# First expert layer of a vision tower: from every expert on every token to gathered tiles of 128 rows

## The chip, the cores and the metric

One core of a Trainium2 chip (trn2) runs the whole model in one launch. The metric is the device time of one execution in microseconds, as the median of several runs. All times below are of that core. Engines: TensorE (PE, with PEld its weight loads), VectorE (DVE), ScalarE (ACT), GpSimd (POOL) and SyncE (SP), which issues nearly all plain DMAs.

## The reference, cut to what matters

The model turns 4 images into 756 tokens of width 192 (`T = 756`, six groups of 126 in the kernel), and then runs two layers, each an attention part and an expert part. The change is in the expert part of the first layer (`L0_ffn`). It normalises the tokens and adds this to them:

```python
H, I, E, K = (192, 384, 7, 2)
def _mlp(x, wg, wu, wd):
    return jax.nn.silu(x @ wg) * (x @ wu) @ wd
# x: (756, 192), fp32
# scores = sigmoid((x @ router_w) * routing_bias); the two largest of 7 per token are kept
# and divided by their sum; a token's result is
#   shared _mlp(x) + sum over its 2 experts of weight * routed _mlp_e(x)
```

So every token needs the shared expert and two of seven routed ones. The second layer's expert part is another mixture (8 experts, two per token, at most 190 tokens each, width 768); in both kernels it gathers its tokens.

## The kernel before

Everything is written out by hand: each engine has its own program (`te` TensorE, `ve` VectorE, `ac` ScalarE, `po` GpSimd, `sp` SyncE), and semaphores join them. PSUM is used as a ring of 8 banks (class `Ring`): `ring.add` lists the fills in order, `take` waits on TensorE until the bank is free and `full` waits on a reader until it is filled. The order of the work on an engine is that of its program.

The first expert part works in this order. `layernorm(3)` on VectorE writes `xn`; TensorE transposes it to `xT` (`tr_pairs("ln1", ...)`) and multiplies with the router (`rt`). VectorE splits `xn` into a part rounded to fp32r and a remainder (`cat`, L1486 and L1488), TensorE transposes both (L715) into `xS`, 3 x 128 rows. `spin` (L483) issues products of the identity with itself that nobody reads. Then a loop over 8 experts (7 routed, the shared one last), two per turn, runs on all engines:

- SyncE loads one expert's gate and up weights (`in_fgu`, 1152 KB, the 192 rows laid twice) into `rawf`, and its down weights (`in_fdn`, 288 KB) into `raw2`. ScalarE rounds `rawf` into `wA` (L1099), and GpSimd writes the remainder into `wB` (L1842). The semaphore `f_split` tells TensorE that the weights are ready and SyncE that `rawf` is free.
- TensorE makes 12 gate and up products of 378 tokens. Each is 3 passes with `wA` and 2 with `wB`, in fp32r. ScalarE takes Silu of the gate (L1105), VectorE multiplies with up (L1516) into `aT`.
- TensorE makes the down product of all six token groups (18 fp32 products of 192 columns, each two passes, 36 in the trace). VectorE adds it to `h`, scaled by the token's weight for this expert (`cw`, L1523). That weight is 0 for a token that did not choose the expert.

`layernorm(4)` follows (L1225, L1228, ...), then 16 spins, the transposes L496, and the second attention (`qk` and so on).

The second layer's expert part is used below as a source of rows. There VectorE ranks the tokens by expert, a product `ix` of one-hot matrices (L928) gives each slot its row number (`row`, L1778), GpSimd gathers rows by indirect DMA from a copy of `xn` in DRAM (L1868, 95 rows each) and scatters results to `yd` (L1873); SyncE loads `yd` back (L457) and VectorE adds it (L1815). Its weights per expert are `in_mfc` and `in_mpj`, 576 KB each.

## Time and profile before

| | |
|---|---|
| median of 3 runs | 578.01 us (577.99 to 584.29) |
| the profiled execution | 581.97 us, its span 580.1 us, mean granted TensorE clock 0.909 |
| PE, PEld busy | 534.2 us (92%), 467.7 us (81%) |
| DVE, ACT, POOL busy | 250.0, 183.1, 79.3 us |
| DMA | 38.07 MB, mean 66 GB/s |

The span runs from the first to the last instruction; 1.87 us of the profiled execution lie around it. Busy time of an engine is the union of its instructions. A granted clock of 1.00 is 2.4 GHz, one of 0.50 is 1.2 GHz.

### The profile page before, as it was taken

To read this page: it belongs to the slowest core of one execution; us is meant where nothing else is said; L and a number is where in the kernel's file an instruction comes from. 1 tells how busy PE (TensorE), PEld (TensorE's weight loads), DVE (VectorE), ACT (ScalarE), POOL (GpSimd) and SP (SyncE) were. 2 spreads that over 40 slices of the span, in tenths; PEclk is the share of its full clock that TensorE was granted. 3 is DMA by queue.
4 is the path that set the end of the run, shared out by engine and by line. 5 is a ranking of instruction groups with operands and counts; after the bars stand their busy time and mean duration, and the time that the engine had idled before them with its cause. 6 is when DMAs were issued, how large, how long until landed. Compare 5 with 4: busy or idle time off the path is not lost. (4 is left out here: it accounts for less than half of the span.)

```text
span 580.1 us, 9334 instructions
## 1 busy us (share of the span) xinstructions
PE 534.2 (92%) x3600; PEld 467.7 (81%) x3600; DVE 250.0 (43%) x700; ACT 183.1 (32%) x344; POOL 79.3 (14%) x79
## 2 busy tenths in 40 slices
PE   6989979999989999999999997899999988899996
PEld 4657969657788899999999976797767657789996
DVE  1561853127467333333333359664233225522114
ACT  2242532213381544325353243231222233212210
POOL 0020000002000220122222000310000000186130
PEclk9997777857899899999999997999979677899999
DMA  8970000000000012222212212012000002065563
GB/s 282 224 201 1 2 1 0 1 0 1 1 1 1 7 77 104 102 102 102 102 65 74 85 42 67 1 34 89 1 3 0 2 1 81 6 162 131 164 202 107
DMA packets 21181, 38.07 MB, mean 66 GB/s; under 512 B 6515, under 2 KB 15261, under 8 KB 20122
## 3 DMA queue, kind: packets, MB, share of 16 engines
q1 hardware_dynamic: 18906, 35.88, 20.4%
q0 software_dynamic: 2240, 1.71, 1.2%
q8 instruction: 24, 0.39, 0.3%
q14 instruction: 11, 0.09, 0.1%
HBM read 33.41 MB, written 4.51 MB: 65 GB/s over the span
## 5 line engine op out<-in xcount | busy, mean ns | idle before, releaser
L478 PE MATMUL bank<-raw,big 128*126 128x192 f32 (+1 forms) x480 | 80.4, 326 | 1.4 <-issue 1.4
L478 PEld LDWEIGHTS bank<-raw,big 128*126 128x126 f32 (+1 forms) x480 | 77.7, 178 | 2.2 <-issue 2.2
L478 PE MATMUL bank<-xS,wA 128*128 128x378 f32 x288 | 66.7, 339 | 0.8 <-POOL wB L1842 0.8
L1516 DVE TENSOR_TENSOR big<-bank,big 128x378 f32<-128x378 f32 x48 | 26.5, 552 | 65.1 <-PE bank L478 47.6
L478 PEld LDWEIGHTS bank<-xS,wA 128*128 128x128 f32 x288 | 51.0, 189 | 1.9 <-issue 1.9
L483 PE MATMUL bank<-ident 128*128 128x128 f32 x328 | 45.5, 305 | 4.7 <-ACT lg L1122 4.0
L483 PEld LDWEIGHTS bank<-ident 128*128 128x128 f32 x328 | 44.5, 220 | 5.5 <-ACT lg L1122 4.5
L1842 POOL TENSOR_TENSOR wB<-raw,wA 128x768 fp32r<-128x768 f32 x16 | 28.7, 1819 | 146.3 <-ACT wA L1099 146.3
L478 PE MATMUL bank<-xS,wB 128*128 128x378 f32 x192 | 48.7, 335 | 0.0
L1105 ACT ACTIVATE big<-bank 128x378 f32<-128x378 f32 x48 | 23.3, 487 | 63.1 <-PE bank L478 63.1
L478 PEld LDWEIGHTS bank<-xS,wB 128*128 128x128 f32 x192 | 34.8, 188 | 0.0
L478 PE MATMUL bank<-big,raw 96*128 96x190 f32 x192 | 32.4, 325 | 1.2 <-issue 0.7
L478 PEld LDWEIGHTS bank<-big,raw 96*128 96x128 f32 x192 | 31.0, 189 | 1.6 <-issue 0.8
L1523 DVE SCALAR_TENSOR_TENSOR h<-bank,cw,h 126x192 f32<-126x192 f32 x48 | 18.6, 415 | 27.4 <-PE bank L478 27.4
L1194 ACT ACTIVATE big<-bank 128x380 f32<-128x380 f32 (+1 forms) x32 | 13.1, 408 | 52.1 <-PE bank L478 51.0
L1159 ACT ACTIVATE big<-bank 128x1000 f32<-128x1000 f32 x12 | 12.0, 1004 | 34.8 <-PE bank L832 34.8
L478 PE MATMUL bank<-big 128*36 128x192 f32 (+2 forms) x88 | 17.7, 365 | 5.2 <-DMA tokb<-in_tokb 5.2
L478 PEld LDWEIGHTS bank<-big 128*36 128x36 f32 (+2 forms) x88 | 12.1, 151 | 10.1 <-DMA tokb<-in_tokb 5.2
L1868 POOL DMA_INDIRECT big<-xd,row x14 | 17.0, 1211 | 24.0 <-DVE row L1787 20.0
L1803 DVE TENSOR_SCALAR big<-bank,wslot 95x192 f32<-95x192 f32 x16 | 6.6, 413 | 28.8 <-PE bank L478 25.8
L478 PE MATMUL bank<-xT,wqq 97*128 97x189 f32 (+1 forms) x96 | 18.7, 356 | 0.3 <-DVE big L1657 0.3
L1099 ACT ACTIVATE wA<-raw 128x768 fp32r<-128x768 f32 x24 | 18.5, 832 | 1.6 <-PE bank L478 1.5
(389 smaller groups left out, 866.8 us busy)
## 6 DMA issues: line engine op xcount, KB each, us to landing
raw<-in_fgu SPq DMA_DIRECT2D x8, 1152.0 KB, 5.2
raw<-in_mfc SPq DMA_DIRECT2D x8, 576.0 KB
raw<-in_mpj SPq DMA_DIRECT2D x8, 576.0 KB
big<-in_w SPq DMA_DIRECT2D x5, 576.0 KB, 7.4
raw<-in_fdn SPq DMA_DIRECT2D x8, 288.0 KB, 5.2
big<-in_p SPq DMA_DIRECT2D x3, 432.0 KB, 4.7
yd<-big SPq DMA_DIRECT2D x1, 1134.0 KB
xd<-xn SPq DMA_DIRECT2D x2, 567.0 KB
```

Source lines behind the costliest of these rows:

```text
L478: mm = te.matmul(o, l, r, start=first and k == 0, stop=last and k == len(pairs) - 1)
L483: te.matmul(ps[:, 0:128], ident[:, :], ident[:, :], start=True, stop=True)
L1099: ac.activation(wA[:, c, :], rawf[:, c, :], ACT.Copy).then_inc(f_wh, 1)
L1105: ac.activation(sg[:, 3 * u + m, :], ps[:, 0:HALF], ACT.Silu).then_inc(emptied_s, 1)
L1159: ac.activation(PT[:, m, :, :], quad(("T", i, m, 0))[:, :, 0:KT], ACT.Exp, scale=float(AD) ** -0.5).then_inc(emptied_s, 4)
L1194: ac.activation(heT[:, e % 2, ms[0]:ms[0] + n, :], ps[:, 0:n * CAP].rearrange("p (q c) -> p q c", q=n), ACT.Gelu).then_inc(emptied_s, 1)
L1516: ve.tensor_tensor(aT[s][:, m, u * HALF:(u + 1) * HALF], ps[:, 0:HALF], sg[:, 3 * u + m, :], ALU.mult).then_inc(emptied_v, 1)
L1523: it = ve.scalar_tensor_tensor(h[:, t, :], ps[0:TT, q * D:(q + 1) * D], cw[:, t, bass.ds(2 * i + s, 1)], h[:, t, :], ALU.mult, ALU.add)
L1803: ve.tensor_scalar(yo[:, z, :], ps[0:CT, 0:D], wslot[:, z:z + 1], None, ALU.mult).then_inc(emptied_v, 1)
L1842: it = po.tensor_tensor(wB[:, c, :], rawf[:, c, :], wA[:, c, :].bitcast(F32), ALU.subtract)
L1868: po.indirect_dma_start(xg[:, z, :], None, xd[:, :], bass.IndirectOffsetOnAxis(row[:, z:z + 1], 0), bounds_check=2 * T - 1, oob_is_err=Fal ...
```

## The change

The seven routed experts are no longer run on all tokens. The 1512 pairs of token and expert are sorted by expert into tiles of 128 slots. An expert may leave its last tile partly empty, so 18 tiles (`NJ`) are laid out, always all 18, whatever the routing. VectorE works out each tile's expert (`eid`) and each slot's token; GpSimd gathers 128 rows per tile (`xg1`), and SyncE reads the expert's number into a register and loads that expert's weights (576 KB and 288 KB) for each tile, into three buffers in turn. The fp32r split is gone, all these products are plain fp32. The shared expert is run on all tokens, before the tiles. Sixteen tiles' results are scattered to DRAM and read back, the last two are put in place by a one-hot product (`cb1`), in one PSUM group with the shared down product of three token groups.

```diff
+TS = 128
+NJ = (2 * T + (FE - 1) * (TS - 1)) // TS
# tensor
-            te.wait_ge(cat_r, 1)
-            for t in range(NT):
-                ps = take(("xs", t))
-                for c in range(3):
-                    mm = te.transpose(ps[:, c * TT:(c + 1) * TT], cat[:, t, c * 128:(c + 1) * 128], ident[0:TT, 0:TT])
...
-            spin(psum[ring.bank(("g", 0, 0, 0))], 24)
-            with te.Fori(0, FE // 2) as i:
-                for s in range(2):
-                    te.wait_ge(f_split, 2 * i + s + 1)
...
-                                acc(take((nm_, s, u, m), i)[:, 0:HALF],
-                                    [(wA[:, c, n], xS[:, c, cs]) for c in range(3)] + [(wB[:, c, n], xS[:, c, cs]) for c in range(2)]
-                                    ).then_inc(bank_full, 1)
+            def shared_pair(u, m):
+                for z, name in enumerate(("sg", "su")):
+                    n = slice(z * FI + m * 128, z * FI + (m + 1) * 128)
+                    acc(take((name, u, m))[:, 0:HALF],
+                        [(up_of[2][:, k, n], xT[0:DH, k, u * HALF:(u + 1) * HALF]) for k in range(2)]).then_inc(bank_full, 1)
+            te.wait_ge(w_up[2], 16)
+            shared_pair(0, 0)
+            shared_pair(0, 1)
+            ps = take("cs1")
+            te.wait_ge(sel1_r, 1)
...
+            shared_pair(0, 2)
+            for m in range(3):
+                shared_pair(1, m)
+            ps = take("ix1")
+            for z in range(2 * NT):
+                if z % 4 == 0:
+                    te.wait_ge(oh1_r, z // 4 + 1)
+                mm = te.matmul(ps[:, 0:3 * NJ], ohj1[:, z, :], ohi1[:, z, :, :], start=z == 0, stop=z == 2 * NT - 1)
...
+            for t in range(3):
+                shared_down(t, True)[1].then_inc(bank_full, 1)
+            def tile_rows(j):
+                ps = take(("tx", j))
+                if j == 0:
+                    spin(ps, 8)
+                te.wait_ge(gat1[j], 16)
+                for k in range(2):
+                    mm = te.transpose(ps[0:DH, k * TS:(k + 1) * TS], xg1[:, j, k * DH:(k + 1) * DH], ident[:, :])
+            def tile_up(j):
+                te.wait_ge(w_up[j % 3], 16 * (j // 3 + 1 + j % 3 // 2))
+                te.wait_ge(*ring.done(("tx", j)))
+                for z, name in enumerate(("tg", "tu")):
...
+                        mm = acc(ps[:, m * TS:(m + 1) * TS], [(up_of[j % 3][:, k, n], xe1[:, j % 2, k, :]) for k in range(2)])
+            def tile_down(j):
+                te.wait_ge(w_down[j % 3], 16 * (j // 3 + 1))
+                te.wait_ge(*ring.done(("tu", j)))
+                acc(take(("td", j))[:, 0:D], [(hT1[:, j % 2, m, :], down_of[j % 3][:, m, :]) for m in range(3)]).then_inc(bank_full, 1)
+            tile_rows(0)
+            tile_rows(1)
+            tile_up(0)
+            for j in range(NJ):
+                if j + 2 < NJ:
+                    tile_rows(j + 2)
+                if j + 1 < NJ:
+                    tile_up(j + 1)
+                tile_down(j)
+            te.wait_ge(oh1c_r, 2)
+            for t in LAST:
+                ps = shared_down(t, False)[0] if t >= 3 else take(("cb1", t))
+                for c in range(2):
+                    te.wait_ge(*ring.done(("td", NJ - 2 + c)))
+                    mm = te.matmul(ps[0:TT, 0:D], oh1c[:, c, t * TT:(t + 1) * TT], yo1[:, NJ - 2 + c, :], start=t < 3 and c == 0, stop=c == 1)
# sync
+            sp.wait_ge(eid_r, 1)
+            for j in range(NJ):
+                chosen = sp.value_load(eid[0:1, j:j + 1], min_val=0, max_val=FE - 2)
+                if j >= 2:
+                    sp.wait_ge(*ring.full(("tu", j - 3) if j >= 3 else ("su", 1, 2)))
+                expert(up_at[j % 3], "fgu", chosen, w_up[j % 3])
+                if j >= 3:
+                    sp.wait_ge(*ring.full(("td", j - 3)))
+                expert(down_at[j % 3], "fdn", chosen, w_down[j % 3])
+            sp.wait_ge(sca1, 16 * (NJ - 2))
+            for u in range(2):
+                ts = slice(3 * u, 3 * u + 3)
+                for k in range(2):
+                    sp.dma_start(yb1[:, k, ts, :], tokens(yd1[k * T:(k + 1) * T, :])[:, ts, :]).then_inc(y1_in[u], 16)
# gpsimd
-                        it = po.tensor_tensor(wB[:, c, :], rawf[:, c, :], wA[:, c, :].bitcast(F32), ALU.subtract)
+            for j in range(NJ):
+                po.indirect_dma_start(xg1[:, j, :], None, xd1[:, :], bass.IndirectOffsetOnAxis(row1[:, j:j + 1], 0),
+                                      bounds_check=2 * T - 1, oob_is_err=False).then_inc(gat1[j], 16)
+            for j in range(NJ - 2):
+                po.wait_ge(*ring.done(("td", j)))
+                po.indirect_dma_start(yd1[:, :], bass.IndirectOffsetOnAxis(row1[:, j:j + 1], 0), yo1[:, j, :], None,
+                                      bounds_check=2 * T - 1, oob_is_err=False).then_inc(sca1, 16)
# vector, after 18 tiles of gate times up (tile_gated) and scaled rows out (tile_rows_out)
+            for u in range(2):
+                ts = slice(3 * u, 3 * u + 3)
+                ve.wait_ge(y1_in[u], 32)
+                for k in range(2):
+                    st(ve.tensor_tensor(h[:, ts, :], h[:, ts, :], yb1[:, k, ts, :], ALU.add))
+                    own()
+            for q in range(NT + 1):
+                if q < NT:
+                    t = LAST[q]
+                    ps = full(("cb1", t))
+                    ve.tensor_tensor(h[:, t, :], ps[0:TT, 0:D], h[:, t, :], ALU.add).then_inc(emptied_v, 1)
+                if q >= 1:
+                    t = LAST[q - 1]
+                    ve.wait_ge(*ring.done(("cb1", t)))
+                    st(ve.bn_stats(bn[:, t, :], h[:, t, :]))
```

`fgu` is now (8, 96, 1536), without the doubled rows. ScalarE copies the transposed rows into `xe1` and takes Silu of 128 x 384 per tile; it no longer rounds weights, and GpSimd no longer subtracts. `xd1` is a DRAM copy of `xn` (two writes of 567 KB), and `yd1` is cleared in DRAM (1134 KB) before the scatters.

How the instructions stand on three engines. First TensorE from the router product on (names: `xT` the transposed tokens, `raw` the weight buffers, `big` in L715 the split tokens and in L779 the one-hot matrices). Before:

```order
L478 MATMUL bank<-rwt,xT 126x7 x11
L715 MATMUL bank<-ident,big 128x126 [waits emptied_v,cat_r]
L715 MATMUL bank<-ident,big 128x126 x2
L483 MATMUL bank<-ident 128x128 [waits emptied_s,emptied_v]
L483 MATMUL bank<-ident 128x128 x23
L720 UNCONDITIONAL_BRANCH
L473 ISA [waits f_split]
L478 MATMUL bank<-xS,wA 128x378 x2
L478 MATMUL bank<-xS,wB 128x378 x2
```

After, up to the first gathered rows and the first tile:

```order
L520 MATMUL bank<-rwt,xT 126x7 x11
L520 MATMUL bank<-xT,raw 128x378 [waits emptied_v,w_up2,ld_moe]
L767 MATMUL bank<-selb,tri 126x56 [waits sel1_r,emptied_s]
L520 MATMUL bank<-xT,raw 128x378 [waits emptied_s]
L779 MATMUL bank<-big 128x54 [waits oh1_r,emptied_s]
L520 MATMUL bank<-raw,big 126x192 [waits emptied_v,w_down3]
L525 MATMUL bank<-ident 128x128 x7
L796 MATMUL bank<-ident,big 96x128 [waits gat1_0]
L796 MATMUL bank<-ident,big 96x128 [waits gat1_1,emptied_v]
L520 MATMUL bank<-mt,raw 128x128 [waits emptied_s,w_up0]
```

The transposes of the split tokens and the 24 spins are gone; the shared expert, the rank and slot products, 8 spins and two waits for gathers stand between the router and the first tile.

Second, SyncE for one expert before (in the loop) and for one tile after:

```order
L402 ISA [waits f_split]
L402 DMA raw1<-in_fgu 128x2304
L430 REGISTER_ALU
L402 ISA [waits bank_full]
L402 DMA raw2<-in_fdn 128x576
```

```order
L464 TENSOR_LOAD eid
L464 ISA x2
L436 ISA [waits bank_full]
L436 DMA raw1<-in_fgu 96x1536
L436 DMA raw2<-in_fdn 128x576
```

A read of `eid` into a register now stands ahead of each pair of loads, and the pair is issued 18 times, where it was 8.

Third, VectorE at the end of the part. Before:

```order
L1523 SCALAR_TENSOR_TENSOR h<-bank,cw,h 126x192
L1211 REGISTER_ALU
L1510 COMPARE_AND_BRANCH
L1225 BN_STATS bn<-h 126x6 [waits emptied_v]
L1228 BN_AGGR mv<-bn 126x2 [waits v_step]
```

After:

```order
L1684 TENSOR_SCALAR big<-bank,wslot 128x192 [waits bank_full] x2
L1695 TENSOR_TENSOR h<-h,ovs 126x576 [waits y1_in0,emptied_v]
L1695 TENSOR_TENSOR h<-h,ovs 126x576 [waits y1_in1,v_step]
L1701 TENSOR_TENSOR h<-bank,h 126x192 [waits bank_full,v_step]
L1705 BN_STATS bn<-h 126x6 [waits emptied_v]
L1326 BN_AGGR mv<-bn 126x2 [waits v_step]
```

Between the last tile and the statistics of `layernorm(4)` there is now a wait for the rows that come back from DRAM (`y1_in`), and six additions of `cb1` behind it.

## Rows read from the trace of the kernel before

**Rows 1.** Busy time by stretch: from:to length, engines (instructions), clock, DMA share, GB/s.
```profile
187.70:201.90 14.20, 12.54 (x95) 11.87 (x94) 6.11 (x17) 9.00 (x14) 3.59 (x2) 0.88 0.01 1
201.90:333.60 131.70, 131.13 (x770) 130.25 (x771) 44.62 (x95) 49.71 (x77) 25.16 (x14) 1.00 0.26 90
333.60:340.10 6.50, 5.40 (x45) 4.41 (x43) 4.78 (x21) 1.95 (x4) 0.00 (x0) 1.00 0.29 91
```
**Rows 2.** Timeline within one expert: start us, us, engine, line, what, count.
```profile
205.10 0.52 PE L478 MATMUL bank<-xS,wB 128*128 128x378 f32 x2
205.45 0.68 PE L478 MATMUL bank<-xS,wA 128*128 128x378 f32 x3
...
212.38 6.01 PE L478 MATMUL bank<-raw,big 128*126 128x192 f32 x36
```
**Rows 3.** Timeline ahead of the first expert.
```profile
191.81 3.53 PE L715 MATMUL bank<-ident,big 126*128 126x126 f32 x18
...
196.06 5.60 PE L483 MATMUL bank<-ident 128*128 128x128 f32 x48 [0.72 <-ACT xS L1092]
```
**Rows 4.** Busy time by stretch, as rows 1, behind the router product.
```profile
192.00:193.00 1.00, 1.00 (x6) 1.00 (x6) 0.57 (x3) 0.53 (x2) 0.00 (x0) 0.50 0.00 0
```
**Rows 5.** Groups by form: line, what, count, busy us, mean ns, idle before.
```profile
L478 PE MATMUL bank<-xT,wp 96*128 96x378 f32 x32 | 10.3, 480 | 0.0
L690 PE MATMUL bank<-ident,big 126*96 126x126 f32 x36 | 4.3, 272 | 1.7 <-DVE big L1452 1.7
```
**Rows 6.** Timeline: fp32 passes of 128 and of 48 columns.
```profile
181.84 3.73 PE L483 MATMUL bank<-ident 128*128 128x128 f32 x32
...
500.81 2.14 PE L928 MATMUL bank<-big 126*95 126x48 f32 x24
```
**Rows 7.** Timeline, second expert part: one-hots, row numbers, gathers, first wait for one.
```profile
497.62 0.36 DVE L1767 TENSOR_TENSOR big<-prd,iota 126x192 f32<-126x192 f32 x1
...
498.55 1.48 DVE L1773 TENSOR_TENSOR big<-prd,iota 126x380 f32<-126x380 f32 x3
...
503.19 0.17 DVE L1778 TENSOR_TENSOR row<-fidx,bank 95x16 int32<-95x16 f32 x1
...
504.46 1.40 POOL L1868 DMA_INDIRECT big<-xd,row  x1 [20.03 <-DVE row L1787]
...
506.17 1.21 POOL L1868 DMA_INDIRECT big<-xd,row  x1 [0.30 <-issue]
...
512.33 0.34 PE L936 MATMUL bank<-ident,big 95*96 95x95 f32 x2 [0.70 <-DMA big<-xd,row]
```
**Rows 8.** Busy time by stretch, second expert part, weight loads beside gathers, then scatters.
```profile
508.00:511.00 3.00, 3.00 (x21) 3.00 (x20) 0.41 (x1) 0.00 (x0) 2.39 (x3) 1.00 0.76 204
...
535.00:543.00 8.00, 7.52 (x46) 7.22 (x45) 0.82 (x2) 1.63 (x4) 3.34 (x3) 1.00 0.83 254
```
**Rows 9.** Timeline: last scatter to `yd`, its load back, the additions.
```profile
556.53 1.11 POOL L1873 DMA_INDIRECT yd<-big,row  x1 [0.84 <-issue]
...
560.81 1.83 SPq L457 DMA_DIRECT2D big<-yd  x4
...
565.43 1.55 DVE L1815 TENSOR_TENSOR h<-h,big 126x576 f32<-126x576 f32 x2 [1.35 <-DMA big<-yd]
...
567.36 1.55 DVE L1815 TENSOR_TENSOR h<-h,big 126x576 f32<-126x576 f32 x2 [0.38 <-DMA big<-yd]
```
**Rows 10.** Timeline: aggregation after the part; additions with statistics after attention.
```profile
335.85 0.51 DVE L1228 BATCH_NORM_AGGREGATE mv<-bn 126x2 f32<-126x6 f32 x6
...
376.90 0.36 DVE L1611 TENSOR_TENSOR h<-bank,h 126x192 f32<-126x192 f32 x1 [0.30 <-PE bank L478]
377.18 0.35 DVE L1614 BATCH_NORM_STATS2 bn<-h 126x6 f32<-126x192 f32 x1
```
**Rows 11.** Timeline and stretch: TensorE after 4 us without work.
```profile
356.24 5.99 PE L483 MATMUL bank<-ident 128*128 128x128 f32 x27 [4.02 <-ACT lg L1122]
...
356.00:362.00 6.00, 5.76 (x27) 5.76 (x28) 5.72 (x12) 0.47 (x2) 0.00 (x0) 0.50 0.13 38
```

More of the change, by code:

```diff
@@ L439, in _ @@
+            sp.wait_ge(*ring.full(("cb1", LAST[-1])))
+            m_load(1, 1, 1)
             sp.wait_ge(*ring.full(("qk", 2, 3)))
             load("wq2", (wq2[0:DH, :, :], a["wq2"]), (wq2[DH:DH + 1, 0, :], a["wq2b"]))
-            load("tok7", (vB[:, :], a["tok7"].partition_broadcast(TT)))
-            tokens = lambda q: q.rearrange("(t p) d -> p t d", p=TT)
             sp.wait_ge(z_set, 1)
@@ new lines, in _, with shared_down @@
+            mm.then_inc(bank_full, 1)
+            shared_pair(0, 2)
[6 more added lines that the diff above has]
+                mm = te.matmul(ps[:, 0:3 * NJ], ohj1[:, z, :], ohi1[:, z, :, :], start=z == 0, stop=z == 2 * NT - 1)
+            mm.then_inc(bank_full, 1)
+            def shared_down(t, last):
+                te.wait_ge(*ring.done(("su", t // 3, 2)))
+                ps = take(("sd", t) if last else ("cb1", t))
+                return ps, acc(ps[0:TT, 0:D], [(aT[:, m, t * TT:(t + 1) * TT], down_of[3][:, m, :]) for m in range(3)], last=last)
@@ L1086, in _ @@
             ac.activation(rstd[:, 0:NT], rstd[:, 0:NT], ACT.Sqrt).then_inc(std_ready, 1)
+            ac.activation(esum[0:1, 3:4], ones[0:1, 0:1], ACT.Sigmoid)
             evac_pairs("ln1", xT)
@@ L1526, in _ @@
-            ve.wait_ge(*ring.done(("dn", 1, 3), FE // 2 - 1))
-            layernorm(4)
+            st(ve.tensor_tensor(before, tri8[:, :].rearrange("p (a b) -> p a b", a=8), ntl.unsqueeze(1).to_broadcast([TT, 8, 8]), ALU.mult))
+            own()
+            st(ve.tensor_reduce(off, before, X, ALU.add))
+            own()
+            ve.scalar_tensor_tensor(place, off.unsqueeze(1).to_broadcast([TT, NT, 8]), float(TS),
+                                    ps[0:TT, 0:48].rearrange("p (t n) -> p t n", n=8), ALU.mult, ALU.add).then_inc(emptied_v, 1)
@@ new lines, in _ @@
+            ve.wait_ge(*ring.done("cs1"))
+            st(ve.tensor_tensor(pay[:, :, 0, :].rearrange("p k (t n) -> p k t n", n=8), place.unsqueeze(1).to_broadcast([TT, 2, NT, 8]),
+                                pick[:, :, :, :], ALU.mult))
+            own()
+            rank, which, prob = (prd[:, v, :] for v in range(3))
+            st(ve.tensor_reduce(rank.rearrange("p (k t) -> p k t", k=2), pay[:, :, 0, :].rearrange("p k (t n) -> p k t n", n=8), X, ALU.add))
+            st(ve.tensor_tensor(end, off, ntl, ALU.add))
@@ new lines, in _ @@
+            own()
+            st(ve.tensor_tensor(ge, bc(rank, [TT, 2 * NT, NJ + 1]), step[:, :].unsqueeze(1).to_broadcast([TT, 2 * NT, NJ + 1]), ALU.is_ge))
+            st(ve.tensor_tensor(past, end[0:1, 0:7].unsqueeze(1).to_broadcast([1, NJ, 7]), bc(iota[0:1, 0:NJ], [1, NJ, 7]), ALU.is_le))
+            own()
+            st(ve.tensor_reduce(eidf[:, :], past, X, ALU.add))
+            st(ve.tensor_reduce(tile_of, ge[:, :, 1:NJ + 1], X, ALU.add))
+            own()
+            st(ve.tensor_scalar(eidf[:, :], eidf[:, :], float(FE - 2), None, ALU.min))
@@ new lines, in _ @@
+            shared_gated(0, 2)
+            for m in range(3):
+                shared_gated(1, m)
+            ps = full("ix1")
+            st(ve.tensor_scalar(fidx1[:, :], ps[:, NJ:2 * NJ], -BIG, BIG, ALU.mult, ALU.add))
+            own()
+            ve.tensor_tensor(row1[:, :], fidx1[:, :], ps[:, 0:NJ], ALU.add).then_inc(row1_r, 1)
+            st(ve.tensor_tensor(late1[:, :], fidx1[:, NJ - 2:NJ], ps[:, NJ - 2:NJ], ALU.add))
+            ve.tensor_copy(wslot1[:, :], ps[:, 2 * NJ:3 * NJ]).then_inc(emptied_v, 1)
@@ new lines, in _ @@
+            ve.wait_ge(*ring.done("ix1"))
+            own()
+            st(ve.tensor_scalar(wrap1[:, :], late1[:, :], float(T), -float(T), ALU.is_ge, ALU.mult))
+            own()
+            st(ve.tensor_tensor(late1[:, :], late1[:, :], wrap1[:, :], ALU.add))
+            own()
+            for t in range(3):
+                ps = full(("sd", t))
+                ve.tensor_tensor(h[:, t, :], ps[0:TT, 0:D], h[:, t, :], ALU.add).then_inc(emptied_v, 1)
+            ve.wait_ge(*loaded("tok7"))
@@ L1529, in products @@
+            own()
+            layernorm(4, stats=False)
             def products(r, ls, ms):
```

261 lines of the change are left out of this document (160 added, 101 removed).

## The prediction

> **What bounds the kernel now.** I read busy time by stretch first, cut at the borders of the first expert part. From 201.9 to 333.6 TensorE is busy 131.13 of 131.70 us at full clock, while VectorE has 44.6, ScalarE 49.7 and the DMA engines a share of 0.26 [rows 1]. So this part is TensorE's own work, nothing is waited for, and the question is how many passes there are at what price. Next I read the timeline inside one expert. Five fp32r passes of 378 columns repeat every 0.87 us (the pair with `wB` starts at 205.10, the next three at 205.45), so a pass is 0.174 us, and the 36 passes of a down product take 6.01 us, 0.167 each [rows 2]. One expert is 12 x 0.87 + 6.01 = 16.45 us, eight are 131.6, and that is the stretch. Ahead of the loop lie the transposes of the split tokens and 24 spins (48 passes, 5.60 us) [rows 3]. The loop's result reaches the aggregation of `layernorm(4)` at 335.85 [rows 10]. I make the sum on that clock: when would this instruction start in the changed kernel?
>
> **Removed.** Everything on TensorE from the end of the router product (191.8, where the transposes start [rows 3]) to the end of the last down product (333.6): 141.8 us. ScalarE's rounding, GpSimd's subtraction and the loop's branches were beside it and give nothing more.
>
> **Added, TensorE.** (1) Shared gate and up: 12 groups of 2 fp32 products, two passes each, 48 passes of 378 columns. The same form costs 10.3/32 = 0.322 us [rows 5], so 15.5 us. fp32 passes are dearer than fp32r (0.174), but there are 4 for 5. (2) The rank product `cs1`, 7 small passes, and the slot product `ix1`, 24 passes of 54 columns: near 2.14/24 = 0.09 us each [rows 6], at most the 0.117 of a 128-column pass. I take 0.6 and 2.5 us. (3) Shared down for three token groups, 18 passes of 192 columns, 3.0 us, and 8 spins, 16 x 3.73/32 = 1.9 us [rows 2, 6]. (4) The tiles. One is 2 transposes at 4.3/36 = 0.12 [rows 5], 24 passes of 128 columns at 0.117 and 6 of 192 at 0.167: 0.24 + 2.80 + 1.00 = 4.04 us. Eighteen are 72.7 us, whatever the routing. (5) `cb1`: 9 products for the other shared rows, 12 one-hot ones, 42 passes of 192 columns, 7.0 us. All together 103.2 us of work against 141.8.
>
> **Where the path has gaps.** At 191.8 TensorE starts the shared expert with no wait (its weights come in with the early loads). In the kernel before, the clock there is 0.50 for some 3 us [rows 4], 18 transposes took 3.53 us where 18 x 0.12 = 2.1 would do [rows 3]. The new passes sit in the same place: +1.6. So `cs1` starts at 191.8 + 16 x 0.322 + 1.6 = 198.6, the other 32 passes of the shared expert end at 209.5, `ix1` at 212.0. VectorE's routing chain must fit between `cs1` and 209.5, 10.3 us: 22 small instructions of 0.15 to 0.45 (192 elements cost 0.36) and three one-hots of 512 elements at 1.48/3 x 512/380 = 0.66 [rows 7], about 8 us with the waits between. I take it as hidden; if not, its rest comes on top one for one.
>
> From `ix1` on nothing hides. Row numbers 0.5 us later; GpSimd's first gather starts 1.27 after the row number does (503.19 to 504.46), the next 1.7 later, then every 1.5 [rows 7]. The first tile's gate product stands behind the transposes of both tiles 0 and 1 in TensorE's queue, so it waits for the second gather. The nearest row has a gather started at 506.17 and TensorE released at 512.33, 6.2 us, beside a weight load of 576 KB [rows 7]. The lower bound is the issue itself, 1.2. Here the first loads are long in, so I take 4.3. Gather 1 starts near 215.4, lands at 219.7; TensorE has 3.0 + 1.9 us of work until 216.9 and then idles but for two transposes. Such a gap costs clock afterwards, and I put 1.7 on it as for the head. Tiles: 219.7 + 72.2 (two transpose pairs are ahead) + 1.7 = 293.6. `cb1` ends at 300.6.
>
> **The tail** is longer than TensorE. Tile 15 is full 4.8 us before the end of tile 17's down, 288.8. VectorE scales it, GpSimd starts its scatter about 1.8 later, 290.6. Then as in the second part: start of the last scatter to SyncE's loads 4.3, to the first addition 4.6, to the end of the additions 3.5 (556.53, 560.81, 565.43, 567.36 + 1.55) [rows 9], which gives 303.0. Six `cb1` additions with statistics follow at 0.65 per group (376.90 to 377.55, the pair of [rows 10]), and the aggregation starts at 306.9. Before it was 335.85: **28.9 us earlier**. One more loss: TensorE's 16 spins end near 304.4, and the next rows come near 308.4, so it idles some 4 us. After such an idle time 27 passes took 5.99 us at clock 0.50 instead of 3.2 [rows 11]; the `qk` products now stand there, and VectorE waits for them. I take 2.4.
>
> **Weights.** Each tile needs 864 KB, 885 kB, in 4.04 us, 219 GB/s, where one expert had 1.47 MB in 16.45 us. While loads and gathers run together the row has 204 GB/s at a share of 0.76, and with scatters 254 at 0.83, each with pauses in it [rows 8]. The next load of a gate buffer is issued when tile j-3's down is full, since it stands behind that wait in SyncE's queue, and is used two tiles later, 8.3 us. Two issues, the register read, and a landing of about 4 to 5 us fit. The register read has no row: its bounds are 0 and, if it were as long as the whole slack, 2 to 3 us, and up to there it costs nothing. The Trainium skill (DMA: Bandwidth & Descriptors, "Latency and other measured facts") gives a `tensor_load` a floor of about 600 ns; by that the sum stays as it is.
>
> **Sum.** 28.9 - 2.4 = 26.5 us. The profiled execution was 581.97 us, which becomes 555.5; the median of the runs stands 3.96 lower, so 578.01 - 26.5 = **551.5 us**.
>
> **Rivals.**
> - *The weights pace the tiles.* If the traffic runs at 204 GB/s [rows 8], a tile with its 98 kB of gathered rows takes 983/204 = 4.8 us in the first seven tiles (+5.4), and 885/204 = 4.34 in the rest (+3.3): 560. For it: share 0.76 to 0.83 with loads half as dense. Against: those rows contain pauses. Chance 0.17.
> - *The way to the first tile is longer*: the chain sticks out, gathers of 128 rows cost more than those of 95, landing takes 6.2 us. +2 each, 557. Chance 0.10.
> - *The clock keeps up.* No loss at the three places (1.6, 1.7, 2.4): 546. Against: [rows 4, 11]. Chance 0.12.
> - *Slower: TensorE starves in each tile and its clock falls.* If loads come late by a microsecond or two per tile, the gap comes 18 times, and passes go at the price of rows 11 (5.99/27 = 0.222 for 128 columns). A tile would then be near 7.8 us at half clock throughout: 72.7 becomes 140, 619 us. It ends above 578 once a tile takes more than 4.04 + 26.5/18 = 5.5 us, so with under half of the passes slow. Against: three buffers and a need of 219 GB/s. Chance 0.04. The Trainium skill (TensorE: Matmul & The Clock Gate, "HAM oscillation") describes this course, a tile loop whose short compute is followed by a DMA wait and starts cold each time; this trace shows only the single case of rows 11.
> - *It does less than it says*: it can't do fewer tiles, since 18 are laid out always, and this is in the sum. A wrong count is no rival.
>
> **Numbers.** My course has 0.55 and spans 548 to 556; 0.02 is left for a cause that I don't see. Range 545 to 566: it holds the clock case, the long way to the first tile and the weight case. A measurement here tells about 2% from no change, 566.4 or below for faster. Faster 0.92, same 0.04, slower 0.04.
>
> **What would show it.** A tile period of 4.0 to 4.1 us on TensorE and no idle time for `raw` loads (else the weight case); a first transpose of gathered rows near 218 and the first gate product of a tile near 220; `ix1` without a wait for VectorE; a clock of 0.50 behind the wait for gathers and after `layernorm(4)`; the aggregation near 307. The prediction is wrong if a tile takes 4.5 us or more, or if parts outside of 188 to 360 us move.

## The result, and the profile after

The changed kernel took 565.68 us (median of 4 runs, 559.62 to 569.55), the kernel before 579.41 us in the runs beside it. The ratio is 0.9725 with an interval of 0.9653 to 0.9797: faster, but by 14 us and not by 26.5. The profiled execution was 569.55 us with a span of 567.8 us, where the prediction had 555.5 for the profiled execution. It is the slowest of the four and counts as one in the chip's slower state, but its mean granted clock of 0.879 is that of the others (0.878 to 0.892), and a second trace (`e1_again`, 567.51 us) looks the same.

I cut the trace at the borders of the changed kernel's own stages. The columns are those of [rows 1].

```profile
193.70:201.10 7.40, 7.40 (x19) 4.22 (x19) 4.19 (x13) 2.49 (x4) 0.00 (x0) 0.70 0.01 3
...
228.00:242.00 14.00, 8.21 (x33) 6.17 (x32) 0.97 (x2) 0.87 (x2) 9.55 (x10) 0.65 0.34 87
242.00:253.30 11.30, 11.30 (x64) 10.97 (x63) 2.42 (x5) 2.12 (x5) 2.40 (x3) 0.68 0.76 202
253.30:307.70 54.40, 52.40 (x424) 50.94 (x422) 13.10 (x27) 12.23 (x26) 12.79 (x13) 1.00 0.84 212
307.70:319.30 11.60, 10.38 (x74) 10.18 (x73) 6.69 (x17) 0.00 (x0) 0.00 (x0) 1.00 0.99 268
```

The fourth row is what was expected of all tiles. The second is what nobody ordered: in 14 us TensorE makes 33 passes where steady tiles would have some 115, VectorE and ScalarE two instructions each, and only GpSimd (9.55 us, 10 instructions) is busy. The DMA engines are not what holds them, at a share of 0.34.

The head of the part, in the timeline. `layernorm(3)` was aggregated at 185.67, 1.0 us later than before (184.67), so 1.0 is to be taken off each clock time here.

```profile
189.91 3.96 PE L520 MATMUL bank<-rwt,xT 96*126 96x7 f32 x24 [0.72 <-issue]
193.72 7.50 PE L520 MATMUL bank<-xT,raw 96*128 96x378 f32 x16
201.06 0.19 PE L767 MATMUL bank<-selb,tri 126*126 126x56 bf16 x1
...
201.43 10.41 PE L520 MATMUL bank<-xT,raw 96*128 96x378 f32 x32
211.68 2.78 PE L779 MATMUL bank<-big 126*128 126x54 f32 x24
...
217.38 1.10 POOL L2024 DMA_INDIRECT big<-xd,row  x1 [0.30 <-issue]
220.18 0.73 PE L796 MATMUL bank<-ident,big 128*96 128x128 f32 x4 [0.95 <-DMA big<-xd,row]
221.12 1.13 PE L520 MATMUL bank<-mt,raw 96*128 96x128 f32 x8 [0.21 <-issue]
```

Sixteen passes of 378 columns take 7.50 us and 32 of them 10.41: the first ones run at half clock. `ix1` starts with no wait behind it. The first gate product stands at 221.12.

Next the place where it breaks. Bracketed is the idle time ahead and what ended it.

```profile
227.97 0.50 PE L520 MATMUL bank<-mt,raw 96*128 96x128 f32 x3
...
228.75 0.72 PE L520 MATMUL bank<-mt,raw 96*128 96x128 f32 x5 [0.28 <-issue]
...
234.46 1.00 POOL L2024 DMA_INDIRECT big<-xd,row  x1 [0.30 <-issue]
234.46 0.37 PE L520 MATMUL bank<-mt,raw 96*128 96x128 f32 x1 [0.61 <-issue]
...
237.32 0.56 DVE L1680 TENSOR_TENSOR mt<-bank,mt 128x384 f32<-128x384 f32 x1 [10.84 <-remote]
...
240.15 0.42 DVE L1684 TENSOR_SCALAR big<-bank,wslot 128x192 f32<-128x192 f32 x1 [2.27 <-remote]
240.28 0.35 SPq L436 DMA_DIRECT2D raw<-in_fdn  x1
...
241.57 0.38 ACT L1189 ACTIVATE mt<-bank 96x256 f32<-96x256 f32 x1 [10.86 <-remote]
```

TensorE gets a few passes out every 0.7 us, with nothing in the profile that it would wait for ("issue"). VectorE stands 10.84 us for a product that was full near 227 and whose Silu ended at 230.7, and SyncE issues `fdn` for tile 3 at 240.28 although tile 0's down product, for which it waits, is in PSUM by 228. Meanwhile GpSimd issues a gather every 1.30 us, the 18 of them from 215.88 to 239.4, and with the last one the others come back. Behind it tile 3's passes run at half clock (0.50 from 235 to 249), which is part of the price. The gate product of tile 2 starts at 227.97, that of tile 5 at 253.55: 25.6 us for three tiles, where the tiles behind show 3.87 each:

```profile
253.55 2.84 PE L520 MATMUL bank<-mt,raw 96*128 96x128 f32 x24
253.66 0.35 SPq L436 DMA_DIRECT2D raw<-in_fdn  x1
...
254.77 0.33 SPq L436 DMA_DIRECT2D raw<-in_fgu  x1
...
256.23 1.14 PE L520 MATMUL bank<-raw,mt 128*128 128x192 f32 x6
...
257.42 2.84 PE L520 MATMUL bank<-mt,raw 96*128 96x128 f32 x24
```

And the tail, to be held against [rows 9] and the first of [rows 10]:

```profile
304.06 0.98 POOL L2028 DMA_INDIRECT yd<-big,row  x1 [2.91 <-DVE big L1684]
...
306.19 1.84 SPq L475 DMA_DIRECT2D ovs<-yd  x4
...
309.02 5.86 SPq L436 DMA_DIRECT2D raw<-in_mpj  x2
...
310.42 1.55 DVE L1695 TENSOR_TENSOR h<-h,ovs 126x576 f32<-126x576 f32 x2 [2.28 <-DMA ovs<-yd]
...
314.45 1.55 DVE L1695 TENSOR_TENSOR h<-h,ovs 126x576 f32<-126x576 f32 x2 [2.48 <-DMA ovs<-yd]
...
319.31 0.51 DVE L1326 BATCH_NORM_AGGREGATE mv<-bn 126x2 f32<-126x6 f32 x6
...
320.96 2.75 PE L538 MATMUL bank<-ident,xn 126*96 126x126 f32 x12 [2.88 <-DVE xn L1333]
324.43 15.47 PE L520 MATMUL bank<-wqq,xT 97*126 97x288 f32 x64 [0.72 <-issue]
```

The aggregation comes 16.5 us earlier than before (319.31 against 335.85), not 28.9. The 64 `qk` passes behind it take 15.47 us where they took 12.12 before, the first of them at half clock. From here to the next aggregation it is 48.8 us (319.31 to 368.13), before it was 44.6 (335.85 to 380.43). From there to the end both kernels take 199.7 us. So the 12.3 us of span are -1.0 (start) + 17.5 (the part) - 4.2 (behind it).

Since the start of the part lies between 183.2 and 195.4 in the profiled runs below, and the untouched stretch behind the second attention takes 192.4 to 200.8 us, whatever the edit, the medians of two kernels can differ by some us for no reason of theirs. I compare kernels by the time from the aggregation of `layernorm(3)` to that of `layernorm(4)`, "the part": 151.2 us before, 133.6 here, 122.2 as predicted (306.9 - 184.67). Each part is read from one trace, and the same kernel gave 133.6 and 132.3, so a difference of 1 to 2 us says nothing by itself.

### The profile page after: what moved, and what is told of

Its sections match the earlier page's. It is cut to its first block and busy times, and to the rows that moved or that the text cites. A ratio compares the mean times of both kernels' runs of the same rounds, so it can differ in the third digit from the quotient of the medians.

```text
span 567.8 us, 8847 instructions
## 1 busy us (share of the span) xinstructions
PE 510.1 (90%) x3497; PEld 430.2 (76%) x3497; DVE 237.3 (42%) x691; ACT 148.3 (26%) x302; POOL 87.6 (15%) x98
## 3 DMA queue, kind: packets, MB, share of 16 engines
q0 software_dynamic: 3872, 4.04, 3.0%
## 5 line engine op out<-in xcount | busy, mean ns | idle before, releaser
L520 PE MATMUL bank<-mt,raw 96*128 96x128 f32 x432 | 57.0, 288 | 6.7 <-issue 4.7
L520 PEld LDWEIGHTS bank<-mt,raw 96*128 96x128 f32 x432 | 53.7, 201 | 9.2 <-issue 5.8
L520 PE MATMUL bank<-raw,big 128*95 128x192 f32 (+1 forms) x228 | 38.9, 327 | 1.4 <-issue 1.4
L520 PEld LDWEIGHTS bank<-raw,big 128*95 128x95 f32 (+1 forms) x228 | 36.6, 167 | 2.2 <-issue 2.2
L1680 DVE TENSOR_TENSOR mt<-bank,mt 128x384 f32<-128x384 f32 x18 | 10.0, 558 | 61.9 <-PE bank L520 47.9
L2024 POOL DMA_INDIRECT big<-xd,row x18 | 18.3, 1017 | 46.8 <-DVE row L1661 41.6
L520 PE MATMUL bank<-raw,mt 128*128 128x192 f32 x108 | 22.8, 349 | 1.3 <-issue 1.2
L2028 POOL DMA_INDIRECT yd<-big,row x16 | 15.8, 988 | 49.9 <-DVE big L1684 47.9
L2054 POOL DMA_INDIRECT big<-xd,row x14 | 16.9, 1207 | 25.6 <-DVE row L1967 21.6
L520 PEld LDWEIGHTS bank<-raw,mt 128*128 128x128 f32 x108 | 18.7, 205 | 1.3 <-issue 1.3
L520 PEld LDWEIGHTS bank<-xT,wqq 97*128 97x128 f32 (+1 forms) x96 | 18.1, 217 | 0.6 <-issue 0.5
```

The lines of the kernel that those rows point to most:

```text
L520: mm = te.matmul(o, l, r, start=first and k == 0, stop=last and k == len(pairs) - 1)
L1680: ve.tensor_tensor(hT1[:, j % 2, :, :].rearrange("p m c -> p (m c)"), ps[:, 0:FI], sg1[:, j % 2, :], ALU.mult).then_inc(emptied_v, 1)
L2024: po.indirect_dma_start(xg1[:, j, :], None, xd1[:, :], bass.IndirectOffsetOnAxis(row1[:, j:j + 1], 0), bounds_check=2 * T - 1, oob_is_err= ...
L2028: po.indirect_dma_start(yd1[:, :], bass.IndirectOffsetOnAxis(row1[:, j:j + 1], 0), yo1[:, j, :], None, bounds_check=2 * T - 1, oob_is_err= ...
L2054: po.indirect_dma_start(xg[:, z, :], None, xd[:, :], bass.IndirectOffsetOnAxis(row[:, z:z + 1], 0), bounds_check=2 * T - 1, oob_is_err=Fal ...
```

## The experiments

**Is the stall the kernel's, and whose?** Four kernels. `e1_again` has no edit.

> The changed kernel once more, unedited. In its first trace all engines but GpSimd stand nearly still from 228 to 242 us, with the 18 row gathers being issued at 215.9 to 239.4. If that stall belongs to the kernel (theories A to C below), it is in this trace too, between tile 2 and tile 4, and costs 8 to 14 us; if it was a single accident, it is gone, the tiles end near 295 and the execution takes about 555 us. Theory A: GpSimd's 18 gathers, issued back to back, hold up the other engines. Theory B: the register reads on SyncE and the weight transfers do. Theory C: the tile loop, written out 18 times where the kernel before had a loop of four turns, is fetched too slowly, whatever else is going on.

566.16 us, part 132.3 us. The stall is there again, at the same place behind the first gather:

```profile
228.00:242.00 14.00, 7.95 (x29) 5.51 (x28) 0.88 (x2) 1.63 (x4) 8.01 (x9) 0.65 0.25 69
```

It is no accident.

`e2_paced`:

```diff
-            for j in range(NJ):
-                po.indirect_dma_start(xg1[:, j, :], ...
+            for j in range(5):
+                gather1(j)
             for j in range(NJ - 2):
                 po.wait_ge(*ring.done(("td", j)))
+                if j + 5 < NJ:
+                    gather1(j + 5)
                 po.indirect_dma_start(yd1[:, :], ...
```

> GpSimd issues only 5 gathers ahead, and each further one when a tile is done (gather j+5 after tile j's product), one by one between the scatters. Theory A: no stall, the first four tiles run at 3.9 us each, tiles end near 294 instead of 307, median about 552. Theories B and C: the stall stays near its place (228 to 242) and the time within 3 us of the changed kernel's 565.

550.4 us (547.19 to 553.06), ratio to before 0.9474 (0.9411 to 0.9537). The part takes 122.5 us. The same stretch in its trace:

```profile
228.00:242.00 14.00, 14.00 (x120) 13.89 (x119) 2.98 (x7) 3.33 (x8) 7.37 (x8) 1.00 0.88 234
```

Theory A: the stall goes by an edit that touches nothing on the other engines. From the first gate product to the last down product it is 74.1 us, where `e1_again` has 84.1. So the way in which GpSimd issues its gathers costs 10 us or more there. The medians lie 15.8 us apart and the two profiled executions 17.4 (567.51, 550.12), but 5.4 of the 17.4 are the untouched stretch at the end (200.4 against 195.1), which other kernels with paced gathers do not repeat (200.8 in `e8_tail`). Pacing by tile has a small price of its own: four waits of TensorE for a gather, 3.0 us together.

`e3_fixed`, which takes fixed experts and leaves out the choice:

```diff
-                chosen = sp.value_load(eid[0:1, j:j + 1], min_val=0, max_val=FE - 2)
+                chosen = j % (FE - 1)
```

> The weights of tile j are those of expert j mod 7, a constant, so that SyncE reads no register; bytes, order and waits are unchanged (the routed experts' results differ). Theory B by the register read: no stall, about 552. Theories A and C: stall as before, within 3 us of 565. The price of the reads themselves in the steady tiles: at most 2 us, by the two waits for weights of 1.7 and 0.2 us.

561.97 us (557.42 to 569.4), part 129.2. The stall stays. VectorE's wait begins at 231.9, 11 us behind the first gather (221.2 here), as in the changed kernel (226.5 and 215.9):

```profile
244.21 0.56 DVE L1680 TENSOR_TENSOR mt<-bank,mt 128x384 f32<-128x384 f32 x1 [12.33 <-remote]
```

In passing it prices the register read. SyncE's two issues are 0.39 us apart here and 1.11 in the changed kernel (253.66, 254.77 above):

```profile
254.37 0.35 SPq L436 DMA_DIRECT2D raw<-in_fdn  x1
254.76 1.05 SPq L436 DMA_DIRECT2D raw<-in_fgu  x1
```

So a read costs 0.72 us. It lies in the slack: in the steady tiles of `e1_again`, with the reads, TensorE has no wait for weights either. The Trainium skill (DMA: Bandwidth & Descriptors, "Latency and other measured facts") gives a `tensor_load` a floor of about 600 ns, and 0.72 us lies just above it.

`e4_noweights`: `for j in range(3)` in place of `range(NJ)` around the weight loads, and the waits on them made constant. It leaves out the weights of all tiles from the fourth on.

> Only tiles 0 to 2 load their weights; the 15 later tiles compute with those three sets (the routed experts' results differ), so 13 MB of transfers and 15 register reads are left out. Theory B: no stall, about 550. Theories A and C: the stall stays, and only the waits for weights in the steady tiles go, 2 us, so about 563.

562.64 us, part 130.2. The stall stays with next to no traffic, at a DMA share of 0.11:

```profile
228.00:242.00 14.00, 8.41 (x25) 5.79 (x25) 1.44 (x3) 1.25 (x3) 7.62 (x9) 0.58 0.11 27
```

Theory B has fallen in both its forms, and what is short in the stall is not DMA bandwidth. Theory C (written-out code) can't be alone, since `e2_paced` has the same code. In the first trace no packet of the queues that the profile calls "instruction" runs between 224.5 and 248.6, so the stall ends without one; no run took the written-out code away, though. Nor are many gathers in a row enough: the second expert part, whose code is written out too, has 14 gathers and 4 scatters in a row in both kernels, without a stall. From the trace of the kernel before, beginning 15 us behind the first of them (504.46 in [rows 7]):

```profile
520.00:524.00 4.00, 4.00 (x27) 4.00 (x26) 0.82 (x2) 0.49 (x1) 3.27 (x3) 1.00 0.61 113
524.00:528.00 4.00, 4.00 (x27) 4.00 (x26) 0.00 (x0) 1.64 (x4) 3.21 (x3) 1.00 0.75 207
```

These are 95 rows every 1.50 us and not 128 every 1.30. They are more DMA packets, not fewer: 480 of GpSimd's queue in these 8 us, 60 per us, against 829 from 216 to 240 in the changed kernel, 35 per us. So it is not the number of packets. This contrast made the next questions.

**What about the gathers is it: their number, their rate, or the empty rows?** `e5_clamped`:

```diff
+            ve.tensor_scalar(rowg[:, :], rowf[:, :], float(2 * T - 1), None, ALU.min).then_inc(row1_r, 1)
...
-                po.indirect_dma_start(xg1[:, j, :], None, xd1[:, :], bass.IndirectOffsetOnAxis(row1[:, j:j + 1], 0),
+                po.indirect_dma_start(xg1[:, j, :], None, xd1[:, :], bass.IndirectOffsetOnAxis(rowg[:, j:j + 1], 0),
```

> All 18 gathers still in a row, but a row number past the end (an empty slot: 792 of the 2304, the last four tiles wholly) is cut to the last row of the table for the gathers alone, so that every gather reads 128 rows; one more small VectorE operation, 0.2 us. Of theory A there are now three forms. A1: what counts is how many rows GpSimd issues without a pause (the queue behind it fills), A2: how fast it issues them, A3: that rows past the end are costly to the other engines. A3: no stall, median about 552. A1 and A2: the stall stays, 565 or some us more.

563.17 us, part 132.3, the stall as before. VectorE's longest wait, from its groups of waits (us in total, times, longest):

```profile
DVE mt L1683 <- remote: 11.5, 1, 11.5
```

The rows past the end don't make it (A3 falls).

`e6_bursts`: `gather1(j)` for 0 to 8 at once, and for 9 to 17 behind the product of tile 1.

> The gathers come in two bursts of 9, the second one behind the product of tile 1 (near 230), the same 1.3 us apart. In four traces the stall begins 12 us behind the first gather, when 9 to 10 are out, and ends with the last. A1: no stall in either burst, and no more than 2 us lost; median 550 to 555. A2 with a short memory, or A3 (the empty rows are nearly all in the second burst): the second burst stalls the engines, at least in its part of four empty tiles, and the time lies above 556.

560.93 us, part 125.2. The first burst (215.0 to 226.8) costs little. The second (231.9 to 243.4, then three scatters as close) has a stall of its own, about half as large. ScalarE, VectorE and TensorE are late from about 236, 238 and 242 on, which is 4, 6 and 10 us after its start; in the changed kernel it is 8, 8 and 12 us after the first gather:

```profile
241.91 0.56 DVE L1680 TENSOR_TENSOR mt<-bank,mt 128x384 f32<-128x384 f32 x1 [6.91 <-remote]
...
246.19 0.37 PE L520 MATMUL bank<-mt,raw 96*128 96x128 f32 x1 [1.10 <-issue]
```

I had expected none by A1 with a row of 9 gathers. But the three scatters follow as closely, so the second row is 12 calls long, and the stall comes 2 to 4 us sooner than behind a fresh start. That a pause of 5 us (with one scatter in it) does not clear what the first burst had built up would fit this and is not shown.

`e7_spaced`:

```diff
+                if 4 <= j < NJ - 1:
+                    if j >= 5:
+                        po.wait_ge(fil, j - 4)
+                    po.memset(big2[:, 1536:2736], 0.0).then_inc(fil, 1)
                 po.indirect_dma_start(xg1[:, j, :], ...
```

> All 18 gathers without a wait for any tile, but from the fifth to the seventeenth GpSimd clears 1200 columns of a free buffer first (about 1.0 us by the memset of 3456 columns in 2.98 us), so that they come some 2.5 us apart instead of 1.3 and the last near 250. A1 in the form of a plain count of gathers: the stall comes after the tenth, near 234, and lasts to 250. A1 in the form of a queue that drains in between, and A2: no stall, 550 to 554. A3: a stall at the empty tiles, from about 240 on.

561.07 us, part 122.5. That is the part of `e2_paced`, but not by the tiles: from the first gate product to the last down product they take 76.8 us against 74.1, and head and tail happen to be 2.7 shorter. Nearly all of the 10.7 us between the medians lies ahead of and behind the part in the profiled executions, and no run explains it. All gathers up to 251.55, 2.28 us apart, pass without a stall: the count alone is not it. But then GpSimd, late with its scatters, catches up with two gathers and seven scatters 1.3 us apart, and a stall comes that nobody had in mind:

```profile
252.86 1.00 POOL L2029 DMA_INDIRECT big<-xd,row  x1 [0.30 <-issue]
...
262.97 0.56 DVE L1681 TENSOR_TENSOR mt<-bank,mt 128x384 f32<-128x384 f32 x1 [8.07 <-remote]
```

Scatters do it as well as gathers. `e10_rows96` and `e11_slower` then separate calls from rows. `e10_rows96`, which leaves out the last 32 slots of every tile, so that the routed results are not those of the model:

```diff
-                po.indirect_dma_start(xg1[:, j, :], None, xd1[:, :], bass.IndirectOffsetOnAxis(row1[:, j:j + 1], 0),
+                po.indirect_dma_start(xg1[0:96, j, :], None, xd1[:, :], bass.IndirectOffsetOnAxis(row1[0:96, j:j + 1], 0),
```

> As the changed kernel, with 18 gathers in a row, but each takes the rows of the first 96 slots alone (the last 32 slots of a tile compute with zeros, so the routed results differ). In the kernel's second layer 14 gathers and 4 scatters of 95 rows follow each other every 1.5 us and nothing stalls; here those of 128 rows every 1.3 us stall all. If the rows per time count, and about 60 to 65 rows per us are worked off: 96 rows per 1.3 us (74 per us) fill the queue slowly, there is no stall or one of 1 to 3 us near the end, and the time is about 552. If the calls per time count, the stall is there as in the changed kernel, 10 to 14 us, and the time 563 to 566.

552.47 us (548.44 to 564.01, the last being the profiled one), part 118.8. Eighteen calls 1.27 us apart, closer than in the changed kernel, and no stall (the gathers are at 225.6 to 248.5, so this is their later half):

```profile
236.00:250.00 14.00, 14.00 (x120) 13.89 (x119) 3.42 (x7) 3.49 (x8) 10.67 (x11) 1.00 0.84 214
```

So calls per time are not it, and rows (or bytes) per time are what is left. `e11_slower`: as `e7_spaced`, with 260 columns from the second gather on.

> As the changed kernel, with 18 gathers of 128 rows, but GpSimd clears 260 columns of a free buffer before each, so that they come every 1.5 us like those of the second layer. If calls per time count: no stall, 552. If rows per time count (85 per us against 60 to 65 worked off): a stall that begins later, after 15 to 20 us (230 to 236), and is shorter, 4 to 9 us; 557 to 561.

553.08 us (547.85 to 558.53), part 118.7. The gathers stand at 221.0 to 247.9; their later half:

```profile
234.00:248.00 14.00, 13.96 (x117) 13.60 (x116) 2.92 (x6) 3.15 (x8) 12.27 (x18) 1.00 0.90 228
```

No stall in this trace either, where I had put 4 to 9 us. So the 60 to 65 rows per us that I had guessed are too few. Together, rows per us of GpSimd's calls: 98 (128 per 1.30) stalls within 8 to 12 us; 85 (128 per 1.50) does not here, 76 (96 per 1.27), 66 (two of 128 per tile) and 63 (95 per 1.50, second part) do not. The last kernel below moves the border.

**The tail.** `e8_tail`, on top of `e2_paced`:

```diff
             sp.wait_ge(*ring.full(("td", NJ - 1)))
+            for u in range(2):
+                sp.wait_ge(y1_in[u], 32)
             for s in range(2):
                 m_load(s, 0, s)
```

> The paced kernel, and SyncE issues the four weight loads of the second layer only when both halves of the routed results have landed. In the paced kernel's trace VectorE starts on the first half at 296.2 and on the second at 301.0, having waited 3.3 us for a transfer that runs beside 2.2 MB of those weights. If those cost it the time, the second half is there when the first has been added (297.8), layernorm(4) comes up to 3.2 us sooner and the median falls from 550.4 to 547 to 548; if the routed results themselves are slow (rows scattered a moment ago), nothing changes. The weights are first used near 480 us, so their delay costs nothing.

549.13 us (542.45 to 551.27), part 117.7 against 122.5. The first row is the second addition of `e2_paced`, the second that of `e8_tail`, which comes when the first half is added:

```profile
301.00 1.55 DVE L1695 TENSOR_TENSOR h<-h,ovs 126x576 f32<-126x576 f32 x2 [3.26 <-DMA ovs<-yd]
```
```profile
296.04 1.55 DVE L1697 TENSOR_TENSOR h<-h,ovs 126x576 f32<-126x576 f32 x2 [0.89 <-DMA ovs<-yd]
```

The wait of 3.26 us falls to 0.89: weights that are needed some 180 us later had been in flight beside the results. From the last scatter to the aggregation it is 13.75 us against 15.99, and these 2.2 us are the edit's. The other 2.5 of the 4.8 lie ahead of that scatter, where the edit changes nothing. The median moved by 1.3 us, with a spread of 9 us in the runs, and can't show it.

**The clock.** `e9_warm`, on top of `e8_tail`: 20 spins for 16 in `tr_pairs("ln1", ...)`, 24 for 16 in `tr_pairs("ln2", ...)`, and

```diff
+            ps = take("rt")
+            spin(ps, 3)
             te.wait_ge(*ring.done(("ln1", 2)))
-            ps = take("rt")
             for t in range(NT):
```

> The kernel with paced gathers and late weight loads, and more warming spins on TensorE: 20 instead of 16 ahead of the transposes for the router, 3 in the 0.72 us ahead of the router's product, and 24 instead of 16 behind the cb1 passes, so that TensorE does not idle 1.6 us before the transposes for qk. In the traces so far the clock is 0.50 from the router's product on for 5 to 7 us and from the first qk passes on for 4 to 10 us. If the idle gaps ahead bring that about: the router's product takes 3.0 instead of 3.9 us, the 64 qk passes 12.2 instead of 15.5, and the median falls from 549.1 by 4 to 6 us to about 544. If it is the thin products themselves (7 columns wide) and the half empty stretch as a whole: within 2 us of 549.

```profile
189.44 2.80 PE L522 MATMUL bank<-rwt,xT 96*126 96x7 f32 x24
192.10 5.33 PE L522 MATMUL bank<-xT,raw 96*128 96x378 f32 x16
...
217.83 4.54 PE L522 MATMUL bank<-mt,raw 96*128 96x128 f32 x24 [0.20 <-issue]
...
306.40 12.12 PE L522 MATMUL bank<-wqq,xT 97*126 97x288 f32 x64 [0.72 <-issue]
```

It was the idle gaps: the thin products are as before, and the clock stays up. The granted clock is 1.00 (2.4 GHz) in all of 184 to 200 and 296 to 320, where `e8_tail` is at 0.50 (1.2 GHz) from 190 to 194 and from 306 to 310; the router's product and the first 16 passes take 8.1 us instead of 11.5, the `qk` passes 12.12 instead of 15.35 in `e8_tail`. The median is 547.57 us (545.62 to 554.63), ratio 0.9418 (0.9298 to 0.9538). That is not to be told from `e8_tail` (549.13 us, ratio 0.9367, 0.9288 to 0.9447), and the expected 544 was missed. Of the 3.4 us won at the head 2.6 are given back before `layernorm(4)` (the part is 116.9 against 117.7), and the trace says where. The first gather starts 3.4 us earlier in the part, but its rows take longer, and no run shows why: from its start to the first transpose it is 4.8 us (212.08 to 216.90) against 3.6 in `e8_tail`, and TensorE waits 1.46 us for it in one piece. Behind this wait the 24 passes of tile 0 take 4.54 us, at a clock of 0.62, where `e8_tail` has 2.84. That is 1.2 and 1.7 us. In return the `qk` stretch is 3.3 us shorter and, as it lies behind all waits for gathers, keeps it.

**All together.** `e12_best`: `e9_warm` with the spaced gathers of `e11_slower`.

> All that helped, in one kernel: 18 gathers in a row but 1.5 us apart (260 columns cleared before each), the second layer's weight loads behind the landed results, and the warming spins. Against the kernel with gathers paced by tiles (aggregation to aggregation 116.9 us in its trace), the waits for a gather that came too late in tiles 9 and 10 (1.3 and 0.6 us) go: 114 to 116 us, median 544 to 547. If GpSimd's gathers and scatters so close together hold up the others again now that the gathers start 3.4 us earlier, a wait of VectorE of over 4 us stands in the trace before 255, and the median is above 549.

553.48 us (550.7 to 554.18), part 121.2, the tiles 77.7 us against 74.0: worse than `e9_warm`, by the second branch of what was expected. The hold-up is back in part:

```profile
236.59 0.56 DVE L1684 TENSOR_TENSOR mt<-bank,mt 128x384 f32<-128x384 f32 x1 [3.80 <-PE bank L799]
...
238.10 0.38 ACT L1192 ACTIVATE mt<-bank 96x256 f32<-96x256 f32 x1 [3.25 <-PE bank L522]
...
242.63 0.56 DVE L1684 TENSOR_TENSOR mt<-bank,mt 128x384 f32<-128x384 f32 x1 [4.85 <-PE bank L522]
...
246.26 0.38 PE L522 MATMUL bank<-mt,raw 96*128 96x128 f32 x2 [0.93 <-issue]
```

In steady tiles these two waits are 2.48 and 2.04. VectorE and ScalarE are thus late by over 1 us from 236 on, 20 us after the first gather (215.90) and while the gathers still come every 1.50 us; TensorE follows at 243, when two gathers and three scatters come 1.3 us apart. So 85 is at the edge and not on the safe side of it. The lowest median is that of `e9_warm`, 18 us below the changed kernel and 34 below the one before; against `e8_tail` it isn't shown to be faster.

## Why the prediction was right in its verdict and 14 us off in its number

565.7 lies in the range of 545 to 566, at its very end, and the verdict is faster. That it lies within is luck: the range was made for the clock, the way to the first tile and the weights, and 14 us came from none of them but from the cause that I didn't see, which had a chance of 0.02. By a sign that the prediction itself gave, a tile of 4.5 us or more, it was wrong: the 18 tiles took 86.6 us, 4.8 each, though a steady one takes 3.87. Point by point, against the prediction's own steps, each moved by the 1.0 us of the later start:

- **What bounds it, and the removed 141.8 us**: right. Nothing else of TensorE's came to be late.
- **The added passes**: right, a little high. 32 passes of 378 columns 10.41 us (0.325 each, 0.322 used), `ix1` 2.78 for 2.5, `cb1` with its waits 6.8 for 7.0. The tile period is 3.87, not 4.04, because consecutive passes of 128 columns start 0.112 us apart (24 in 2.68, 253.55 to 256.23) and not 0.117: 3 us less over 18 tiles.
- **Head clock, +1.6**: right in kind, too small. `cs1` came 1.5 us behind its step (201.06 against 198.6 + 1.0), and `ix1` ended as much later. The router's product itself was slower than before (3.96 us against 3.03), which the step had not counted; that is 0.9 of the 1.5. `e9_warm` gives 3.4 us for both together.
- **VectorE's routing chain hidden**: right, `ix1` did not wait.
- **Way to the first tile**: 221.12 against 219.7 + 1.0. From the start of gather 1 to the gate product it is 3.7 us for 4.3, which made good for part of a late start (217.38 against 215.4 + 1.0). TensorE idled 0.95 us there and not near 2.8, and the clock loss of 1.7 did not come. In `e9_warm`, behind a wait of 1.46 us, it is 1.7 (4.54 - 2.84); that the digits agree is chance.
- **Tiles, 73.9 us from the first gate product to the last down**: the step that failed. It took 86.6 (221.12 to 307.68). Of the excess of 12.7, the stall of tiles 2 to 4 is 14.0 (25.6 - 3 x 3.87), and late weights are 2.8 (three periods of 5.84, 4.30 and 4.28 us between scatters, in which TensorE's two waits are 1.9 of the 2.8). The shorter period takes 3.0 off and the clock loss that did not come 1.7, and 0.6 are left over. The prediction said of the gathers only when the first ones land. It took GpSimd's other 16 as work beside, that costs nobody anything, and neither priced nor bounded that; its sum has them at nothing without a reason. `e1`, `e3`, `e4` and `e5` keep the stall while other suspects are taken away; in `e2`, `e10` and `e11` it is gone, and in `e7` gone from these tiles, by nothing but the pace or the size of the calls.
- **Weights**: right. A DMA share of 0.84 at 212 GB/s carries the steady tiles at a loss of 2.8 us in all, where the rival had 8.7 (5.4 and 3.3). Its 560 would have been nearer to the result for a wrong reason. The register read is 0.72 us, in the slack. By the code a gate buffer's load stands behind the down product of tile j-4, not j-3; the two tiles of slack are the same.
- **The starving rival** (619 us, clock at half throughout): its consequence came for 20 us, not its cause. TensorE starved, and the clock was at 0.50 from 235 to 249. It was GpSimd and not the loads, and it ended with the last gather.
- **The tail**: the total is right (16.3 us from scatter to aggregation, measured 15.25, or 11.6 for 13.3 from the last down product on), its terms are not: SyncE issued 2.1 us after the scatter's start and not 4.3, additions are 0.52 per group and not 0.65, and the second half waited for transfers of later weights, which the prediction had not seen. `e8_tail` takes most of that wait away.
- **Clock behind `layernorm(4)`, 2.4**: right in kind, too small: the stretch is 4.2 longer, 3.35 of them in the `qk` passes (15.47 against 12.12), and the idle time ahead of it was 2.9 us, not 4.

By the clock of the span: 555.5 + 1.0 (start) + 12.7 (tiles) + 0.4 (head) - 1.7 (tail and `cb1`) + 1.8 (behind) = 569.7, against 569.55.

**What stays open**: by which way GpSimd's calls hold TensorE, ScalarE, VectorE and SyncE. It takes 8 to 12 us at 98 rows per us to show, and it is not a want of DMA bandwidth (share 0.11 in `e4_noweights`) nor the number of packets. That something fills and drains is a picture that fits and that no run shows. The Trainium skill (DMA: Bandwidth & Descriptors, "SWDGE vs HWDGE vs iDMA") has GpSimd append a pair of descriptors per DMA operation to rings in SBUF, which the DMA engines then drain. A ring that fills would fit the course in time, and would fit that scatters count like gathers. But by that alone GpSimd itself should be held, and it issues undisturbed every 1.30 us; no run here looked at the rings. Rows and bytes were not told apart by a run, since every row has 768 bytes; but in `e1_again` GpSimd's queue moves 0.01 MB from 236 to 240, in the gathers of the empty tiles, and the stall goes on to 241, so it is not the bytes that move at that moment. Whether written-out code is needed for the stall was not tried. Nor was it settled why 85 rows per us passed in one kernel and not in the other.

## What to carry to other kernels

When an engine off the critical path gets a long run of work at once, such as gathers, look for what the other engines do during that run, and ask for each of its instructions when it is needed: five gathers ahead and one more per tile were worth 10 to 12 us in the tiles (74.1 us against 84.1 and 86.6). Order transfers by first use, also across parts: the weights of a later part cost the routed results 2.4 us. A few spins in gaps of 0.7 to 1.6 us kept TensorE at full clock for the stretch behind, but measure the whole, since part of it was given back at the next wait.

## What was not expected of the hardware

- Indirect transfers of 128 rows issued by GpSimd every 1.30 us slow TensorE, after some 10 us, to about two instructions per us and leave VectorE without one for 11 to 14 us and SyncE for 14 to 15, with no wait of theirs in the profile but "issue" and "remote", until the run ends. It happened in five of five traces with such a run of 18, and not with 96 rows every 1.27 us.
- A call of 128 rows keeps GpSimd for 1.00 us, one of 96 rows for 0.96 (`e10_rows96`) and one of 95 for 1.20 ([rows 7] has 1.21), so the time of a call hardly goes by its rows.
- A register read on SyncE is 0.72 us, and the next load stands behind it.
